# Layer 1's probabilities: from tensor-engine transposes to vector-engine blocks and transfers

## What is computed

```python
q = (x @ Wq + bq).reshape(b, n, H, HD)
k = (x @ Wk + bk).reshape(b, n, H, HD)
v = (x @ Wv + bv).reshape(b, n, H, HD)
q = w_q * q * rsqrt(mean(q * q, -1) + EPS)
k = w_k * k * rsqrt(mean(k * k, -1) + EPS)
scores = einsum('bnhd,bmhd->bhnm', q, k) / sqrt(HD)
attn = softmax(scores)
out = einsum('bhnm,bmhd->bnhd', attn, v).reshape(b, n, H * HD) @ Wo + bo
```

## Time and profile before

| | before |
|---|---|
| time, median of 3 runs | 3258.07 us (3256.71 to 3260.59) |
| the profiled execution | 3259.28 us, its span 3257.5 us |
| granted clock of the tensor engine, mean | 0.991 |
| PE busy | 3165.4 us, 97% of the span |
| DVE busy | 2067.9 us, 63% |
| ACT busy | 1388.4 us, 43% |
| POOL busy | 972.3 us, 30% |
| moved by DMA | 145.32 MB |

### The profile page before, as it was taken

The page is one execution under the profiler, slowest core; times in us unless marked ns, Lnnn a source line. Parts: engine busy times, 40 slices in busy tenths (PEclk is TensorE's granted clock), DMA queues, the critical chain, the costliest instruction groups (busy, mean ns, idle before and its releaser), DMA issues. The chain is left out here.

```text
span 3257.5 us, 58748 instructions
## 1 busy us (share of the span) xinstructions
PE 3165.4 (97%) x19680; PEld 2888.2 (89%) x19680; DVE 2067.9 (63%) x3445; ACT 1388.4 (43%) x2375; POOL 972.3 (30%) x819
## 2 busy tenths in 40 slices
PE   7999999999999978999999999999999999997998
PEld 7989989989989857999999999999999999996786
DVE  3445444455454457777777777777777777776555
ACT  3333333333333323555555555555555555554221
POOL 3333333333333322222222222222222222211765
PEclk9999999999999989999999999999999999999999
DMA  4122122122122101000000000000000000002541
GB/s 128 50 61 60 48 61 60 48 61 60 48 61 60 35 23 34 32 16 31 15 31 15 31 15 31 16 30 24 22 30 16 31 15 31 15 7 79 160 140 55
DMA packets 127177, 145.32 MB, mean 45 GB/s; under 512 B 15488, under 2 KB 91280, under 8 KB 126992
## 3 DMA queue, kind: packets, MB, share of 16 engines
q1 hardware_dynamic: 126272, 143.77, 14.7%
q10 hardware_dynamic: 816, 0.79, 0.1%
q0 software_dynamic: 32, 0.02, 0.0%
HBM read 125.63 MB, written 2.10 MB: 39 GB/s over the span
## 5 line engine op out<-in xcount | busy, mean ns | idle before, releaser
L1304 ACT ACTIVATE b_prob<-b_s_ps,b_shift,b_rstd 128x1024 f32<-128x1024 f32 x252 | 304.2, 1207 | 580.9 <-DVE b_shift L1466 580.9
L1464 DVE TENSOR_REDUCE b_row_max<-b_s_ps 128x1 f32<-128x1024 f32 x252 | 307.2, 1219 | 78.5 <-PE b_s_ps L84 78.4
L82 PE MATMUL b_pj_kq<-b_w_hi,xT_hi 128*128 128x384 f32 x1008 | 341.5, 339 | 1.2 <-DVE b_nat L1434 1.2
L84 PE MATMUL b_pj_kq<-b_w_hi,xT_lo 128*128 128x384 f32 x1008 | 341.9, 339 | 0.0
L83 PE MATMUL b_pj_kq<-b_w_lo,xT_hi 128*128 128x384 f32 x1008 | 341.5, 339 | 0.0
L506 ACT ACTIVATE a_sig<-a_pj 128x512 f32<-128x512 f32 x192 | 114.8, 598 | 486.7 <-PE a_pj L84 486.7
L82 PE MATMUL a_pj<-b_w_hi,xT_hi 128*128 128x256 f32 x1024 | 295.5, 289 | 11.7 <-DVE xT_lo L647 11.1
L84 PE MATMUL a_pj<-b_w_hi,xT_lo 128*128 128x256 f32 x1024 | 289.9, 283 | 0.0
L83 PE MATMUL a_pj<-b_w_lo,xT_hi 128*128 128x256 f32 x1024 | 289.4, 283 | 0.0
L1236 POOL TENSOR_TENSOR b_rstd<-b_mean_sq,power 128x4 f32<-128x4 f32 x128 | 128.9, 1007 | 527.7 <-DVE b_mean_sq L1444 524.4
L1390 PE MATMUL b_t_ps<-ident,b_prob 128*128 128x128 f32 x2048 | 265.6, 273 | 4.8 <-ACT b_prob L1304 4.4
(11 more groups left out here) (272 smaller groups left out, 9107.6 us busy)
## 6 DMA issues: line engine op xcount, KB each, us to landing
b_w_raw<-in_w SPq DMA_DIRECT2D x32, 768.0 KB, 4.3
b_w_raw<-in_w SPq DMA_DIRECT2D x95, 256.0 KB, 3.2
a_k_raw<-a_k_blocks SPq DMA_DIRECT2D x512, 32.0 KB, 1.8
a_w_raw<-in_w SPq DMA_DIRECT2D x32, 256.0 KB, 2.7
a_ow_raw<-in_ow SPq DMA_DIRECT2D x32, 256.0 KB, 3.1
b_ow_raw<-in_ow SPq DMA_DIRECT2D x32, 256.0 KB, 4.5
m_raw_w<-in_mlp_w SPq DMA_DIRECT2D x28, 256.0 KB, 3.0
m_raw_z<-in_mlp_z SPq DMA_DIRECT2D x28, 256.0 KB, 3.8
```

The costliest lines, as they stand in the source:

```text
L82: pe.matmul(out, w_hi, x_hi, start=first, stop=False)
L84: return pe.matmul(out, w_lo, x_hi, start=False, stop=last)
L1304: act.activation(prob[:, :], score_banks(h, t)[:, :], ACT.Exp, bias=shift[:, t:t + 1], scale=rstd[b][:, t, 1:2], accum_out=row_sum[:, t:t ...
L1464: dve.tensor_reduce(row_max[:, t:t + 1], score_banks(h, t)[:, :], AX_X, ALU.max).then_inc(max_done, 1)
```

## The change

Scores now have two pairs of banks, and `prob` two buffers, used by even and odd tiles. The maximum is negated in the same operation and the small one is gone; queries are scaled together with the keys on DVE, so the exponential has no scale. The tensor engine's transposes and `t_ps` are gone. In their place DVE transposes each tile of `prob` in blocks of 32x32 into `blocks` (`transpose_blocks`); after the second tile of a pair SP moves them to their rows with sixteen transfers of 32 rows of 2 KB into `pT_lo` (`move`), which holds the full values at that point; ACT copies the high part to `pT_hi` in two halves (`prob_hi`), and POOL subtracts it in place, in two halves (`prob_lo`). The layout of `pT_hi` and `pT_lo` has four groups of 32 columns outermost, so a matmul's 256 columns are four runs of 64; ACT and DVE put them back in order when they take the value product out. The two halves of a value product are moved two slots later, and stand next to each other on PE: half 0 at the end of an odd slot, half 1 at the start of the next. Output products come two slots later, too, and the weights are split in slots 1, 2 and 4. The core of the diff, in the order SP, POOL, ACT (two functions), PE (two) and DVE:

```diff
+        def move(h, i):
+            sp.wait_ge(blocked, NT * h + BATCH * (i + 1))
+            to = f(pT_lo[i % 2][:, :, :, :])
+            for a in range(GROUPS):
+                for g in range(GROUPS):
+                    sp.dma_start(to[a * BLK:(a + 1) * BLK, g].rearrange("p m n -> p (m n)"),
+                                 blocks[i % 2][g * BLK:(g + 1) * BLK, a].rearrange("p m u q -> p (m u q)")).then_inc(
+                        moved[i % 2], 16)
...
+        def prob_lo(h, i, part):
+            pool.wait_ge(pT_hi_done, 2 * NB * h + 2 * i + part + 1)
+            cut = slice(part * NT // 2, (part + 1) * NT // 2)
+            pool.tensor_tensor(pT_lo[i % 2][:, :, cut, :], f(pT_lo[i % 2][:, :, cut, :]), f(pT_hi[i % 2][:, :, cut, :]),
+                               ALU.subtract).then_inc(pT_lo_done, 1)
...
+        def prob_hi(h, i, part):
+            act.wait_ge(moved[i % 2], MOVED * (2 * h + i // 2 + 1))
             wait(act, pv, NB * h + i - 1)
+            cut = slice(part * NT // 2, (part + 1) * NT // 2)
+            act.activation(pT_hi[i % 2][:, :, cut, :], f(pT_lo[i % 2][:, :, cut, :]), ACT.Copy).then_inc(pT_hi_done, 1)
         def exponent(h, b, t):
             act.wait_ge(shift_done, NT * h + t + 1)
-            wait(act, p_tr, NT * h + t)
-            act.activation(prob[:, :], score_banks(h, t)[:, :], ACT.Exp, bias=shift[:, t:t + 1],
-                           scale=rstd[b][:, t, 1:2], accum_out=row_sum[:, t:t + 1]).then_inc(exp_done, 1)
+            wait(act, blocked, NT * h + t - 1)
+            act.activation(prob[t % 2][:, :], s_ps[t % 2][:, :], ACT.Exp, bias=shift[:, t:t + 1],
+                           accum_out=row_sum[:, t:t + 1]).then_inc(exp_done, 1)
...
         def values(h, b, i, part):
+            pe.wait_ge(pT_lo_done, 2 * NB * h + 2 * i + part + 1)
             if part == 0:
-                pe.wait_ge(pT_lo_done, NT * h + BATCH * (i + 1))
                 pe.wait_ge(v_lo_done, NB * (h + 1))
...
         def step(h, b, cur, rest, nxt, more):
             for s in range(NT):
+                if s % 2 == 0 and quarter(h, b, cur, rest, s):
+                    values(*quarter(h, b, cur, rest, s))
                 if projected(h, b, nxt, more, s):
                     project_tile(*projected(h, b, nxt, more, s))
-                if quarter(h, b, cur, rest, s):
-                    values(*quarter(h, b, cur, rest, s))
                 if nxt and s % 2:
                     transpose_kq(h + 1, s // 2)
-                if rest and s == 0:
-                    transpose_probs(h - 1, NT - 1)
-                if cur and s:
-                    transpose_probs(h, s - 1)
                 for t in scored_in(h, cur, s):
                     scores(h, b, t)
                 if output(h, b, cur, rest, s):
                     output_tile(*output(h, b, cur, rest, s))
+                if s % 2 and quarter(h, b, cur, rest, s):
+                    values(*quarter(h, b, cur, rest, s))
...
+        def transpose_blocks(h, t):
+            i, u = t // BATCH, t % BATCH
+            dve.wait_ge(exp_done, NT * h + t + 1)
+            if u == 0:
+                wait(dve, moved[i % 2], MOVED * (2 * h + i // 2))
+            dve.transpose(blocks[i % 2][:, :, :, u, :].rearrange("p a m q -> p m a q"),
+                          prob[t % 2][:, :].rearrange("p (m a q) -> p m a q", a=GROUPS, q=BLK)).then_inc(blocked, 1)
```

More of the change, by code:

```diff
@@ L1097, in l1_attention @@
         v_lo = [sb(f"v_lo{b}", [P, NT, HD], F32R) for b in range(2)]
-        prob = sb("prob", [P, TOK])
-        row_max = sb("row_max", [P, NT])
+        prob = [sb(f"prob{i}", [P, TOK]) for i in range(2)]
+        blocks = [sb(f"blocks{i}", [P, GROUPS, NT, BATCH, BLK]) for i in range(2)]
         shift = sb("shift", [P, NT])
@@ L1110, in l1_attention @@
         bo_sb = sb("bo_sb", [P, D])
-        s_ps = bank("s_ps", [P, TOK])
-        t_ps = bank("t_ps", [P, TOK])
+        s_ps = [bank(f"s_ps{i}", [P, TOK]) for i in range(2)]
         pj_kq = bank("pj_kq", [P, TOK])
@@ L1117, in l1_attention @@
         y_ps = bank("y_ps", [P, HALF])
-        ln_banks = [s_ps[:, 0:HALF], s_ps[:, HALF:], t_ps[:, 0:HALF], t_ps[:, HALF:]]
+        ln_banks = [s[:, j * HALF:(j + 1) * HALF] for s in s_ps for j in range(2)]
         w_lo_done, proj = aw.lo_done, aw.proj
@@ L1209, in load_output_weights, with step @@
                 sp.dma_start(ow_raw[:, :], ow[ds(h, 1)].rearrange("a p d -> (a p) d")).then_inc(ow_in, 16)
[L1211 to L1215, removed]
+            def move(h, i):
[6 more added lines that the diff above has]
+                            moved[i % 2], 16)
+            def step(h, b, cur, rest, nxt, more):
+                if cur and more:
+                    aw.load(sp, w, h + 2)
+                    load_bias(h + 2, b)
+                if rest:
+                    move(h - 1, NB - 1)
+                if cur:
+                    move(h, 0)
+                if nxt:
+                    load_output_weights(h + 1)
+                if cur:
+                    move(h, 1)
+                    move(h, 2)
             load_bias(0, 0)
@@ L1221, in _ @@
             sp.dma_start(bo_sb[:, :], bo.partition_broadcast(P)).then_inc(const_in, 16)
[L1222 to L1226, removed]
+            steps(sp, step)
             sp.wait_ge(pv, NB * HEADS - 1)
@@ L1375, in scores @@
                     pe.wait_ge(kq_lo_done, NB * (h + 1))
-                wait(pe, exp_done, NT * h + (t - 1 if peeled(h, HEADS - 1) and t else t))
+                wait(pe, exp_done, NT * h + t - 1)
                 cut = slice(t * P, (t + 1) * P)
@@ L1380, in scores @@
                     keys = slice(j * HALF, (j + 1) * HALF)
[L1381 removed]
+                    last = three_pass(pe, s_ps[t % 2][:, keys], q_hi[b][:, cut], q_lo[b][:, cut],
                                       k_hi[b][:, keys], k_lo[b][:, keys], True, True)
                 last.then_inc(scored, 1)
[L1385 to L1391 removed]
             def output_tile(h, b, t):
```

117 lines of the change are left out of this document (52 added, 65 removed).

## The result

| | before | after |
|---|---|---|
| time, median of 4 runs each | 3257.82 us | 3318.06 us (3309.22 to 3324.06) |
| ratio | | 1.0181, 95% interval 1.0152 to 1.0211 |
| the profiled execution | 3259.28 us | 3324.06 us, its span 3322.2 us |
| PE busy | 3165.4 us, 97% | 2993.8 us, 90% |
| POOL busy | 972.3 us, 30% | 1582.9 us, 48% |

A forecast was written before the change was run, and what follows sets the result against it. The tensor engine bounded the kernel before; after it, a ring through several engines at 13.6 us a pair. 3259.3 + 21 (ring) + 12 (end) = 3292, as a median 3291 us; range 3230 to 3520.

The forecast's parts named there:

- the ring: Dependence chain from second value half through project tile, vector engine, ScalarE and GpSimd's subtraction back to itself: 13.6 us a pair, +21 us.
- its own case: The ring sets the period at 13.3 to 13.9 us a pair: 3255 to 3335 us, chance 0.60.
- Where PE waits: Tensor engine idle between the two value halves, released by GpSimd's probability subtraction: about 1.8 us a pair.
- The covers: Transfers (11.4 us with 2.3 spare), block transposition, doubled score banks and reordered value-product operands fit in slack or cost nothing.
- The clock: Idle time in every pair could lower the tensor engine's granted clock; given no chance of its own.
- The end: From last maximum to last output: 26.8 us or more against 16.0 before, taken as +12 us.
- SP as the bound: Rival: issues with 2 KB rows at 1.0 us each make SP need 65.8 us a head, +375 us; chance 0.10.
- The lock: Rival: with sooner transfers GpSimd's subtraction blocks the scaling 1.5 to 2.4 us; 15.1 to 16.0 a pair, about 3510 us; chance 0.13.
- The shorter ring: Rival: GpSimd's half subtraction at 1.3 us, not 2.40, gives a ring of 12.5 us a pair, 3156 us; chance 0.17.
- every ring below 11.84: Far end of the shorter-ring rival: all rings under the 11.84 us a pair of tensor work left, 3068 us.

The follow-up runs named there:

- e1: The changed kernel with the project tile moved ahead of the second value half on the tensor engine in even slots: 3222.66 us, ratio 0.9885 to before.
- e3: The changed kernel with both edits of order, e1 and e2: 3090.26 us, ratio 0.9479 to the kernel before.
- e4: The changed kernel with the two parts of a pair's probabilities cut 5 to 3 blocks of keys, not 4 to 4: 3240.51 us, ratio 0.9941 to before.
- e2: The changed kernel with the maximum ahead of the block transposition on the vector engine in odd slots, except the last head: 3315.87 us, ratio 1.0174 to before.
- e6: The changed kernel with eight transfers of 4 KB rows a pair for sixteen of 2 KB, some blocks in wrong rows: 3502.76 us, ratio 1.0743 to before.
- e9: e6 with one wait more: in even slots GpSimd's first half subtraction waits for the vector engine's scaling; 3294.81 us, ratio 1.0114 to before.

## Why the prediction came out as it did

Its forecast, slower by the ring, held, and so did its own case. The size was 33 us, where the medians differ by 60 and the profiled executions, which are added up here, by 64.8; the profiled one of the changed kernel is the slowest of its four.

- **The ring**, 13.6 us a pair: 13.64. The steps: half subtraction 2.40 forecast and 2.38 measured, block transposition 1.16 and 1.15, exponential 1.19 and 1.10 (now without a scale), value half 1.43 and 1.51 with the restart. The longer copy hand-over (1.21 for 1.03 + 0.04, because GpSimd is still busy with the values' low part) and the shorter exponential nearly cancel, which is luck; e1 to e3 show that the ring itself is real. The period is 0.86 us a head longer; over 28 steady heads that is +24, forecast +21.
- **Where PE waits**: before the second value half, 1.69 us a pair, released by the subtraction; forecast 1.8.
- **The covers** held: sixteen issues take 10.03 us, the doubled scaling 0.68, the value product on runs of 64 shows 2006.34 - 2004.83 = 1.51 for 12 matmuls, of which 0.1 is restart.
- **The clock was the step that failed.** I gave it no chance of its own because a stretch with 8.80 of 10 us busy had kept its level. One stretch was no ground for that: the same kind of stretch kept its level in some places and traces and not in others, and in the first heads it was granted 0.83. By the bias adds above the start cost 12.5 us, some 9 of them by the clock. One more such stretch at 2500 to 2550 made the two heads there 60.67 + 56.23 by the weight loads, in place of 109.1: 7.8 us. Together the clock is 17 us of this execution, a term that the sum had at nothing; the two faster runs of the changed kernel (3309 and 3312 us) had a mean granted clock of 0.987, the two slower ones 0.984 and 0.985.
- **The end was mis-sized**: from the start of the last maximum to the end of the last output 16.0 us before and 33.3 now, +17.3; the sum had 26.8 and I took +12. The rows, DVE:

```profile
3016.76 1.19 DVE L1491 TENSOR_REDUCE b_shift<-b_s_ps 128x1 f32<-128x1024 f32 x1
...
3024.03 0.42 DVE L1511 TENSOR_TENSOR b_o_lo<-b_o_ps,b_o_hi 128x256 fp32r<-128x256 f32 x1 [3.55 <-ACT b_o_hi L1331]
3024.37 1.24 DVE L1499 STREAM_TRANSPOSE b_blocks<-b_prob 128x1024 f32<-128x1024 f32 x1
...
3049.27 0.75 DVE L1520 SCALAR_TENSOR_TENSOR x_nat<-b_pj_kq,b_row_inv,x_nat 128x512 f32<-128x512 f32 x1
```

The last block transposition ends at 3025.61, 8.9 us after the maximum's start, where the sum had 3.7: it stands behind the low part of an output, which waited 3.55 us for ScalarE. SP, still with the pair ahead, was 1.3 us late on top: 26.8 + 5.2 + 1.3 = 33.3. From +12 to +17.3 is 5 us; another 2 lie in the last head. 12.5 + 24 + 7.8 + 17.3 + 2 = 63.6, of 64.8. The +12 itself was a little above the sum's own 26.8 - 16.0 = 10.8.
- **Rivals.** SP as the bound: no, its issues cost 0.63 each with 2 KB rows, as with 1 KB. The lock: not in this kernel, but where the prediction put it; sooner transfers (4.95 us of issues for a pair in place of 10.03) brought 61.43 us a head, against the forecast 15.1 to 16.0 a pair, 60.4 to 64 a head. That it fell in this range is half luck: the scaling was held for 0.97 us on the mean, not 1.5 to 2.4, and 0.78 more came on the tensor engine with the lower clock. The shorter ring needed an edit of order, e1 or e4. That PE then went only to 11.83 with a second edit, e2, the prediction's "every ring below 11.84" had left open.

## What to carry to other kernels

When work leaves the bound, add up the loops of dependence that go through several engines' queues, step by step and start to start; the longest one is the new period, and here it was right within 0.04 us of 13.64, with two errors of about 0.1 us that nearly cancelled. If the bound engine then waits at one place, look first for independent work behind that place on its own queue and move it ahead: one pair of lines changed places on each of two engines, and 1.8% slower became 5.2% faster (e3, 3090.26 us). An edit without effect alone may be half of the gain, so try it again with the first limit gone.

## What the runs showed of the hardware

- The scaling, a vector operation on two SBUF operands, took 1.96 and 2.46 us for 0.68 when it met a running GpSimd subtraction, and ended 0.55 us after it. A block transposition and a maximum were not held: beside the subtraction at 2010.66 they took 1.24 and 1.19 us, as without. The Trainium skill says (SBUF — State Buffer, "Who interferes with whom") that a vector instruction with two SBUF inputs contends with a GpSimd instruction that reads SBUF, and one with at most one SBUF input, outside the 2-port modes, does not; these rows agree. By the order of starts sooner transfers made the kernel 185 us slower, held scaling and lower clock together (e6).
- The issue of an SBUF to SBUF transfer on SP takes 0.62 to 0.63 us for 32 rows of 1, 2 or 4 KB alike (10.12 for sixteen, 10.03 for sixteen, 4.95 for eight).
- The granted clock of PE fell from 1.00 (2.4 GHz) to means of 0.83 and 0.84 over 10 us, which mix its two levels of 2.4 and 1.2 GHz, in a stage that was 87% busy with a wait in every pair, and rose again by itself. How often differs from run to run and is not ordered by the busy share: stretches of 10 us below 1.00 from 1600 to 2600 are 5 of 100 in the changed kernel (87% busy), 10 in e4 (93%), none in e1 (94%), none in e9 (88%), and 42 in e6 (83%), whose stage had a mean of 0.94. The changed kernel's times spread over 15 us, e3's over 5.
